# One kernel, two edits: SBUF tensors moved onto one 512-byte residue, and the pair sums of an attention block folded in two groups of four

## The reference, cut to what matters

```python
def layer_0(y, t):                       # t: the condition, one row per batch
    y = y + gate_a * s5(ln(y) * (1 + scale_a) + shift_a)     # a linear scan over the sequence
    z = (ln(y) * (1 + scale_c) + shift_c) * (1 + scale_ff) + shift_ff
    return y + gate_ff * (gelu(z @ W1 + b1) @ W2 + b2)

def layer_1(hidden, w):
    h = gamma * ln(hidden) + beta
    q, k, v = split(h @ Wqkv.T + bqkv)                       # 16 heads of 32
    att = softmax(q @ k.T, axis=-1) / 512 ** 0.5
    h1 = (att @ v) @ Wp.T + bp + hidden
    return gamma * ln(h1) + beta + h1
```

## Time and profile before

| what | value |
|---|---|
| median of 3 runs | 3031.26 us (3030.69 to 3031.43) |
| the profiled execution's own time | 3036.4 us |
| its span, first to last instruction | 3034.6 us |
| mean granted TensorE clock | 0.983 |
| TensorE busy | 2934.6 us, 97% |
| GpSimd (POOL) busy | 1799.5 us, 59% |
| stretch of the 29 attention blocks that follow the first two | 1406.7 to 2867.7 us |

### The profile page before, as it was taken

How to read it: one execution, slowest core, us unless ns; L and a number is a source line. 1 busy time by engine, 2 the same in 40 slices (tenths; PEclk the granted TensorE clock), 3 DMA queues, 4 the chain that set the end, 5 groups by cost and what they waited for, 6 DMA issues and landing times.

```text
span 3034.6 us, 41281 instructions
## 1 busy us (share of the span) xinstructions
PE 2934.6 (97%) x15018; PEld 1926.7 (63%) x15018; DVE 2000.1 (66%) x3558; ACT 1516.3 (50%) x2756; POOL 1799.5 (59%) x795
## 2 busy tenths in 40 slices
PE   4899999999999998999999999999999999999997
PEld 2787788888888887755555555555555555555456
DVE  6873322222223555688888888888888888888539
ACT  3552233232333221156666666666666666666644
POOL 2776210011110432158888888889888888888854
PEclk7899999999999999999999999999999999999999
DMA  5433100000001567485668865688665778565658
GB/s 214 169 139 125 42 29 1 28 29 28 28 28 42 211 218 218 170 181 119 134 140 178 181 136 126 138 179 166 150 139 122 164 170 178 126 136 125 157 169 295
DMA packets 154074, 404.37 MB, mean 133 GB/s; under 512 B 11621, under 2 KB 29545, under 8 KB 133398
## 3 DMA queue, kind: packets, MB, share of 16 engines
q0 software_dynamic: 22608, 164.64, 27.1%
q1 hardware_dynamic: 131272, 237.15, 25.3%
HBM read 144.51 MB, written 92.31 MB: 78 GB/s over the span
## 4 chain that ended last, share of the span: by engine, by line
PE 54%; DVE 1%; DMA 1%; ACT 1%; issue 0%; SPq 0%; DVEq 0%; ACTq 0%
PE psum L1705 18%; PE psum L1690 16%; PE psum L1717 16%; PE psum L1745 3%; DMA p_att_lo<-att_parts 1%; DVE p_h L2130 0%; PE psum L36 0%; PE psum L38 0%; PE psum L37 0%; ACT probs L1796 0%; DVE p_stats L2136 0%; DVE p_h L2124 0%; DVE p_var L2147 0%; PE psum L1696 0%; DVE part_max L1825 0%
## 5 line engine op out<-in xcount | busy, mean ns | idle before, releaser
L1796 ACT ACTIVATE probs<-psum 128x512 f32<-128x512 f32 x2048 | 1053.7, 610 | 557.9 <-PE psum L1705 555.3
L1825 DVE TENSOR_REDUCE part_max<-psum 128x1 f32<-128x512 f32 x1984 | 1218.3, 679 | 123.9 <-PE psum L1690 118.4
L1940 POOL TENSOR_TENSOR pair<-probs 128x2048 f32<-128x2048 f32 x255 | 1193.8, 4712 | 155.0 <-ACT probs L1796 152.6
L1705 PE MATMUL psum<-queries,keys 97*128 97x512 f32 x2048 | 850.8, 417 | 7.1 <-ACT probs L1796 3.4
L1690 PE MATMUL psum<-keys,queries 96*128 96x512 f32 x1984 | 803.0, 406 | 2.6
L1705 PEld LDWEIGHTS psum<-queries,keys 97*128 97x128 f32 x2048 | 387.3, 190 | 342.2 <-issue 214.6
L1717 PE MATMUL psum<-probs,values 128*32 128x512 f32 x4096 | 500.1, 606 | 0.0
L1690 PEld LDWEIGHTS psum<-keys,queries 96*128 96x128 f32 x1984 | 377.6, 190 | 124.4 <-DVE part_max L1825 45.7
L1077 DVE TENSOR_TENSOR h_lo<-w_stage,h_hi 128x512 fp32r<-128x512 f32 x128 | 98.5, 770 | 497.9 <-ACT h_hi L986 497.9
L979 ACT ACTIVATE w_stage<-psum,b_col 128x512 f32<-128x512 f32 x128 | 88.2, 689 | 492.5 <-PE psum L38 491.7
L1717 PEld LDWEIGHTS psum<-probs,values 128*32 128x32 f32 x4096 | 107.7, 110 | 237.3 <-ACT probs L1796 138.3
(11 more groups left out here) (335 smaller groups left out, 3715.0 us busy)
## 6 DMA issues: line engine op xcount, KB each, us to landing
pair<-pair POOLq DMA_DIRECT2D x157, 1024.0 KB, 7.3
queries<-q_parts SPq DMA_DIRECT2D x96, 256.0 KB, 5.2
keys<-k_parts SPq DMA_DIRECT2D x42, 512.0 KB, 9.9
s_x<-in_x_dram SPq DMA_DIRECT2D x8, 1024.0 KB, 7.7
s_y<-in_x_dram SPq DMA_DIRECT2D x8, 1024.0 KB, 5.4
y_rows<-s_y SPq DMA_DIRECT2D x8, 1024.0 KB, 4.8
q_parts<-qk_hi SPq DMA_DIRECT2D x32, 256.0 KB, 2.0
q_parts<-qk_lo SPq DMA_DIRECT2D x32, 256.0 KB, 2.3
```

The costliest lines, as they stand in the source:

```text
L1705: nc.tensor.matmul(psum[:, SC + unit % 3, :], keys[place(count)[0]][0:R + 1, h, kt * P:(kt + 1) * P], queries[count % NQ][0:R + 1, h, :], ...
L1796: act.activation(probs[tile % NPROB][:, h, :], psum[:, SC + unit % 3, :], ACT.Exp).then_inc(exp_ready, 1)
L1825: dve.tensor_reduce(part_max[:, h * TT + qt, kc:kc + 1], max_slot(), AX.X, ALU.max).then_inc(max_read, 1)
L1940: pool.tensor_tensor(pair[number % NPAIR][:, :, :], probs[2 * number % NPROB][:, :, :], probs[(2 * number + 1) % NPROB][:, :, :], ALU.add) ...
```

## The change

`GROUPS` in `attention_stage` now makes two groups of four pairs in each block but the last, (0,1,2,3) and (4,5,6,7). So a block has six folds, in two chains of three, and two totals. `DIRECT`, `FOLDS` and `SUMMED_AT` follow from it. The last block keeps its four groups of two.

Everything else moves tensors. Small ones are put behind the big ones or padded, so that the big operands of all stages start at the same residue modulo 512 bytes as `raw_weight`. No other instruction changes.

```diff
+OPERAND_STEP = 128
 # s5_stage: the small tensors are handed in, made ahead of the big ones with a pad
-    d_gated = sb("d_gated", [P, B, KT])
-    stats, moment = sb("stats", [P, TT, 6]), sb("moment", [P, TT, 2])
-    var, root, rough, square, inv, off = (sb(f"ln_{n}", [P, TT]) for n in ("var", "root", "rough", "square", "inv", "off"))
+    d_gated, stats, moment = s5["d_gated"], s5["stats"], s5["moment"]
+    var, root, rough, square, inv, off = (s5[n] for n in ("var", "root", "rough", "square", "inv", "off"))
 # ffn_stage
+    NH = 2
+    h_hi = [sb(f"h_hi{n}", [P, CH], F32R) for n in range(NH)]
+    h_lo = [sb(f"h_lo{n}", [P, CH], F32R) for n in range(NH)]
+    u = [sb(f"ffn_u{n}", [P, CH]) for n in range(2)]
     stats = sb("ffn_stats", [P, TT, 6])
...
 # qkv_stage
-    b_col = sb("bqkv_col", [P, 2 * KT])
+    b_col = sb("bqkv_col", [P, OPERAND_STEP])[:, :2 * KT]
     norm = sb("qkv_norm", [P, TT, D])
+    u_hi, u_lo = ([ahead[f"u_{n}"], sb(f"qkv_u_{n}1", [P, KT, CH], F32R)] for n in ("hi", "lo"))
+    u = [sb(f"qkv_u{n}", [P, CH]) for n in range(2)]
     stats = sb("qkv_stats", [P, TT, 6])
...
 # attention_stage
-              for group in (((0, 1, 2), (3, 4, 5), (6, 7)) if count < BLOCKS - 1 else ((0, 1), (2, 3), (4, 5), (6, 7)))]
+              for group in (((0, 1, 2, 3), (4, 5, 6, 7)) if count < BLOCKS - 1 else ((0, 1), (2, 3), (4, 5), (6, 7)))]
...
+    sb("att_pad", [P, OPERAND_STEP - HD])
     keys = [first["keys"]] + [sb(f"keys{b}", [P, HG, L], F32R) for b in range(1, B)]
...
-    ones = sb("att_ones", [P, HD])
     probs = [sb(f"probs{n}", [P, HG, CH]) for n in range(NPROB)]
     pair = [sb(f"pair{n}", [P, HG, CH]) for n in range(NPAIR)]
+    ones = sb("att_ones", [P, HD])
 # project_stage
-    sb("p_between", [P, HG * TT * NCH + 3 * 32 + 2 * D])
+    sb("p_between", [P, HG * TT * NCH + 3 * 32 + 2 * D + OPERAND_STEP - HD])
 # cond_seq_kernel, ahead of s5_stage's big tensors
+                s5["d_gated"], s5["stats"], s5["moment"] = own("d_gated", [P, B, KT]), own("stats", [P, TT, 6]), own("moment", [P, TT, 2])
+                s5.update({n: own(f"ln_{n}", [P, TT]) for n in ("var", "root", "rough", "square", "inv", "off")})
+                own("s5_pad", [P, OPERAND_STEP - 3 * HD])
```

More of the change, by code:

```diff
@@ L727, in ffn_stage @@
     gate = ahead["gate"]
+    NH = 2
+    h_hi = [sb(f"h_hi{n}", [P, CH], F32R) for n in range(NH)]
+    h_lo = [sb(f"h_lo{n}", [P, CH], F32R) for n in range(NH)]
+    u = [sb(f"ffn_u{n}", [P, CH]) for n in range(2)]
     stats = sb("ffn_stats", [P, TT, 6])
     root, inv, off, mean2, var, diff = (sb(f"ffn_ln_{n}", [P, TT]) for n in ("root", "inv", "off", "mean2", "var", "diff"))
-    u = [sb(f"ffn_u{n}", [P, CH]) for n in range(2)]
     u_hi, u_lo, b1_rows = ahead["u_hi"], ahead["u_lo"], ahead["b1_rows"]
@@ L734, in ffn_stage @@
     g = [stage[2][:, n, :] for n in range(2)]
-    NH = 2
-    h_hi = [sb(f"h_hi{n}", [P, CH], F32R) for n in range(NH)]
-    h_lo = [sb(f"h_lo{n}", [P, CH], F32R) for n in range(NH)]
     gated = [stage[2][:, 2 + n, :] for n in range(2)]
@@ L1193, in qkv_stage @@
     bqkv_ones = sb("bqkv_ones", [P, P], F32R)
-    b_col = sb("bqkv_col", [P, 2 * KT])
+    b_col = sb("bqkv_col", [P, OPERAND_STEP])[:, :2 * KT]
     norm = sb("qkv_norm", [P, TT, D])
+    u_hi, u_lo = ([ahead[f"u_{n}"], sb(f"qkv_u_{n}1", [P, KT, CH], F32R)] for n in ("hi", "lo"))
+    u = [sb(f"qkv_u{n}", [P, CH]) for n in range(2)]
     stats = sb("qkv_stats", [P, TT, 6])
     root, inv, off, mean2, var, diff = (sb(f"qkv_ln_{n}", [P, TT]) for n in ("root", "inv", "off", "mean2", "var", "diff"))
-    u = [sb(f"qkv_u{n}", [P, CH]) for n in range(2)]
-    u_hi, u_lo = ([ahead[f"u_{n}"], sb(f"qkv_u_{n}1", [P, KT, CH], F32R)] for n in ("hi", "lo"))
     NO = 4
```

## The result

The changed kernel takes 3236.05 us (median of 4 runs, 3229.55 to 3239.16), the kernel before 3030.98 in the same comparison. The ratio is 1.0669, with a 95% interval of 1.0652 to 1.0686: 205 us slower. I had forecast 95 us slower, 3126 us in a range of 3048 to 3210. The direction held, and so did the chain of waits on POOL. The size was off by a factor of two, because of the loads that meet a fold.

What follows compares the result with a forecast made beforehand. TensorE, busy 97% of the span, was taken as the bound, with POOL setting attention blocks after the change. 84 + 35 - 8 - 16 = +95 us gave a median of 3126 us, range 3048 to 3210.

Steps and rivals of the forecast that it cites:

- TensorE's side: In attention, each of 31 blocks loses one total of 0.86 us, 26.7 us in all, worth nothing once POOL sets the block.
- The order on POOL: In attention blocks, four waited folds instead of two make POOL set the block: +2.7 us each, +84 us over 31 blocks.
- account of 53.05 us a round: POOL's distances between fold issues in an attention block, summed: 7.8 + 23.4 + 11.55 + 10.3, against TensorE's 49.5 us.
- The slack at the start: At attention's start, POOL may fall 7.8 us behind before ScalarE stops: -8 us once.
- Loads that meet a fold: In six key-loading attention blocks, loads lengthen waited folds by some 5.8 us: +35 us, half of the bounds 0 and 70.
- heavy rival: In attention, query loads at every block's end also meet a waited fold: +78 us, 3204 us; chance 0.20.
- The aligned operands: Equal residues speed products in the feed-forward, q, k, v and state-space stages: -16 us, bounds 0 and -22.
- Rival 1: In attention, landings stay under cover and TensorE goes on setting the block: 2987 us; chance 0.09.
- Rival 2: In attention, landings take 6.9 us and key loads miss the waited flights: +19 us, 3050 us; chance 0.14.
- Rival 4: The moved tensors' residues are worth nothing: 3142 us, inside the range; no chance of its own given.
- rival 5: POOL's loss and the gains cancel, which needs a POOL round of 51.1 us: no change; chance 0.03.

Runs made afterwards that it cites:

- mixed kernel: Against the kernel before: tensors moved, groups of four in nine blocks without key loads, with the normalise before pair 6 there; 3013.07 us, ratio 0.995.

## Why the prediction was wrong

*TensorE's side: right.* A total less shortens TensorE's work by 0.86 us, seen in the mixed kernel's blocks of 49.5 us, and is worth nothing where POOL sets the pace.

*The order on POOL: right.* Four waited folds take the cover away. The account of 53.05 us a round was measured at 53.3 with the loads cut. In time, the waits by themselves cost 3112.36 - 3019.53 = 93 us, where the prediction had 84 - 8 = 76. The slack at the start is there: with both loads cut blocks 0 to 2 took 157.6 us on TensorE, for 158.3 in the kernel with its tensors moved alone. But the last of the 31 blocks gave it back, with 56.2 us for 48.3, and the 27 between took 53.4 each, 0.4 more than the account.

*The step that failed is "Loads that meet a fold".* It took +35 us, half of the six blocks' key loads, and left the query loads to the heavy rival. The runs give 3236.05 - 3112.36 = 124 us: 74 for keys and values, 48 for queries. Both halves of every key load hit a waited fold, and each query load did too. I had spread the loads evenly over the block, as if they came at random. They don't. SP issues them when TensorE reaches the middle and the end of a block, and these points stand at a nearly fixed place in POOL's round. In the changed kernel the first half of the keys comes 3.1 to 3.2 us ahead of pair 2's fold in all six blocks, and the second half 1.6 to 3.1 us behind the issue of pair 5's.

The rows of before had half of this. There too all twelve key loads met a fold: the first half came 0.6 to 2.4 us ahead of pair 2's, as in the earlier trace rows, the second ahead of pair 7's, and these folds took 12.3 to 14.6 us to land. No next fold waited for any of these, because pairs 2 and 7 were the last of their groups. The change made pair 2's fold a waited one, so the cost of that half could have been read ahead. And as POOL fell behind TensorE, the second half slid from pair 7's fold, for which no next fold waits, to pair 6's, for which one does. My bound of 70 us for all 12 key loads was near the 74 measured; it was the choice within the bounds that failed, and the query loads that it left out. I had worked out that place for the rival ("pair 5's fold about when TensorE finishes the block") and gave it a chance of 0.20 instead of a term.

*The aligned operands: nearly right.* 11 us measured for 16. The twelve products went from 2.81 to 2.72 us as taken, and the stretch with the h products shrank by 9 us where 11 were taken. Where the rest of the forecast went isn't shown. The Trainium skill (SBUF — State Buffer, "Who interferes with whom") gives TensorE two independent read ports and says that it never waits on anyone, by which the move would be worth nothing. The kernel with only its tensors moved is faster by more than its interval, so the measurement decides against that. No run shows whether a port or something else is behind it.

*The sum.* 93 + 124 - 11 = +206 us, for 205 measured. These are differences of one chain of medians, so they add up by construction. They show where the miss of 110 us sits: 89 us in the loads (124 for 35), 17 in the waits and 5 in the alignment.

*The rivals.* Rival 1 (landings under cover) is out: of 188 folds none landed in under 6.9 us. Rival 2, the light form, is out, as the key loads met waited folds. Rival 4 (the residues are worth nothing) is out by the 11 us, and rival 5 (no change) by the time. Rival 3, the heavy form, 3204 us, was the nearest of all and still 32 us short, in part by luck: its key loads were 39 us, its waits 17 and its alignment 5 on the short side, and its query loads, 78 us for 48 measured, made 30 of that good.

## What to carry to other kernels

Before you add work to an engine that isn't the bound, add up its round with every in-queue wait in it, not its busy time: POOL was 59% busy and had 3.9 us of slack in 50. Then ask which flight each other transfer meets in the trace of before, and who waits for that flight after the change. Here a load met the same flight in every block. A term of that sort is priced at one end or the other, not in the middle. And when one engine falls behind another, redo the places, because a transfer issued by the one slides along the work of the other.

## What the runs showed of the hardware that I had not expected

- Products of 128x512 in this operand format follow each other in 227 ns when the starts of both operands are 0 or 256 bytes apart modulo 512, and in 233 to 234 ns at 64 and at 352 bytes (2.72, 2.80 and 2.81 us for twelve). A common shift of 128 bytes changes nothing. What is behind it stays open.
- In attention the score and search products, with equal residues, still follow each other in 230 ns or more in the kernel with its tensors moved alone, and its blocks went only from 50.3 to 50.6 us to an even 50.3. Why is open.
- A 1 MB accumulating DMA within SBUF lands after 6.9 us at best, and in the changed kernel after 13.3 to 16.2 us in the twelve cases where 1.5 MB of keys were issued ahead of it.
